# Marking runs of nodes with four bfloat16 operations on VectorE instead of one fp32 operation, in a graph network kernel

## The reference

```python
h = relu(layernorm(x))                                          # (50000, 128)
rel_in = concat([h[src_edges], h[dst_edges], edge_attr], -1)    # (25000, 384)
rel = relu(rel_in @ re_w1 + re_b1) @ re_w2 + re_b2              # (25000, 128)
agg = segment_sum(rel, dst_edges, num_segments=50000)           # (50000, 128)
out = x + relu(concat([h, agg], -1) @ ea_w1 + ea_b1) @ ea_w2 + ea_b2
```

## Time and profile before

| | |
|---|---|
| median of 3 runs | 955.37 us (955.33 to 955.7) |
| the profiled execution | 956.01 us, of which the span of the trace is 954.1 us |
| PE busy | 923.3 us (97%) |
| DVE busy | 740.1 us (78%) |
| ACT busy | 605.5 us (63%) |
| POOL busy | 609.1 us (64%) |
| granted clock of PE, mean | 0.987 |

### The profile page before, as it was taken

How to read it: one execution, slowest core, us unless ns; L and a number is a source line. 1 busy time by engine, 2 the same in 40 slices (tenths; PEclk the granted TensorE clock), 3 DMA queues, 4 the chain that set the end, 5 groups by cost and what they waited for, 6 DMA issues and landing times.

```text
span 954.1 us, 21049 instructions
## 1 busy us (share of the span) xinstructions
PE 923.3 (97%) x6450; PEld 817.8 (86%) x6450; DVE 740.1 (78%) x2155; ACT 605.5 (63%) x1180; POOL 609.1 (64%) x600
## 2 busy tenths in 40 slices
PE   4879999999999999999999999999999999999987
PEld 4668998898898899889889889988988988998876
DVE  5887788788788878878877887886887788788562
ACT  1447666666666766666666676666666667666653
POOL 7785776776677677677667767767766776772320
PEclk7979999999999999999999999999999999999999
DMA  6253655555565565555556556555555655554442
GB/s 200 75 148 113 183 163 168 150 177 175 151 186 168 151 183 163 168 151 176 172 155 185 167 153 183 162 169 158 169 174 151 186 167 152 169 177 146 124 123 76
DMA packets 114105, 151.88 MB, mean 159 GB/s; under 512 B 17984, under 2 KB 70080, under 8 KB 113984
## 3 DMA queue, kind: packets, MB, share of 16 engines
q1 hardware_dynamic: 101440, 124.73, 43.2%
q0 software_dynamic: 12544, 25.72, 10.2%
HBM read 104.92 MB, written 45.46 MB: 158 GB/s over the span
## 4 chain that ended last, share of the span: by engine, by line
PE 94%; DVE 3%; SPq 1%; issue 1%; ACT 1%; DMA 0%; DVEq 0%
PE l_ps L531 33%; PE l_ps L546 27%; PE l_ps L536 17%; PE agg_ps L496 7%; PE edge_ps L479 4%; PE node_ps L487 4%; PE node_ps L471 1%; SPq L294 0%; DVE rel_row L831 0%; DVE hot L844 0%; SPq L300 0%; DVE lo L804 0%; DVE h L797 0%; DMA drow_i<-in_dst_rows 0%; DMA win<-rel_rows 0%
## 5 line engine op out<-in xcount | busy, mean ns | idle before, releaser
L386 POOL DMA_INDIRECT gath<-in_x,dst_all x196 | 200.2, 1022 | 59.7 <-issue 59.7
L386 POOL DMA_INDIRECT gath<-in_x,src_all x196 | 195.0, 995 | 52.9 <-issue 51.7
L546 PE MATMUL l_ps<-w2n,hid 128*128 128x128 f32 x1568 | 193.6, 277 | 0.0
L655 ACT ACTIVATE hid<-l_ps,b1n 128x512 f32<-128x512 f32 x196 | 135.0, 689 | 82.4 <-PE l_ps L536 82.4
L409 POOL TENSOR_TENSOR ea_lo<-ea_in,ea_hi 128x512 fp32r<-128x512 f32 x45 | 74.3, 1651 | 171.6 <-ACT ea_hi L629 171.6
L546 PEld LDWEIGHTS l_ps<-w2n,hid 128*128 128x128 f32 x1568 | 182.9, 192 | 0.1
L810 DVE SCALAR_TENSOR_TENSOR lo<-node_ps,hi 128x512 fp32r<-128x512 f32 x98 | 67.3, 687 | 146.1 <-ACT hi L638 146.1
L663 ACT ACTIVATE h<-xin,shift,rs 128x128 f32<-128x128 f32 x392 | 165.2, 486 | 0.0
L531 PE MATMUL l_ps<-hi,w1n_hi 128*128 128x512 f32 x392 | 155.7, 397 | 0.4 <-ACT hid L655 0.4
L531 PE MATMUL l_ps<-hi,w1n_lo 128*128 128x512 f32 x392 | 155.4, 396 | 0.0
L402 POOL TENSOR_TENSOR xb<-xin,b2n 128x512 f32<-128x512 f32 x98 | 131.0, 1354 | 33.5 <-DVE res L838 33.5
(11 more groups left out here) (98 smaller groups left out, 1566.1 us busy)
## 6 DMA issues: line engine op xcount, KB each, us to landing
win<-rel_rows SPq DMA_DIRECT2D x392, 98.0 KB
xin<-in_x_tiles SPq DMA_DIRECT2D x98, 256.0 KB, 4.2
out<-res SPq DMA_DIRECT2D x98, 256.0 KB, 3.4
rel_rows<-rel_row SPq DMA_DIRECT2D x49, 392.0 KB, 2.4
ea_in<-in_ea_t SPq DMA_DIRECT2D x49, 256.0 KB, 3.2
gath<-in_x,src_all POOLq DMA_INDIRECT x196, 2.7
gath<-in_x,dst_all POOLq DMA_INDIRECT x196, 2.9
w1e<-in_L_gnn_re_w SPq DMA_DIRECT2D x1, 384.0 KB, 3.6
```

Of the source, the lines that this page charges most:

```text
L386: nc.gpsimd.indirect_dma_start(gath[b][:, s, k, :], None, x, bass.IndirectOffsetOnAxis(ap=idx[:, e * T + k:e * T + k + 1], axis=0)).then_i ...
L546: last = nc.tensor.matmul(l2_ps[turn % 2][:, k * P:(k + 1) * P], hid[r][:, c, k * P:(k + 1) * P], w[:, c, :], start=(c == 0), stop=(c == C ...
L655: nc.scalar.activation(hid[r][:, c, :], l1_ps[c][:, :], ACT.Relu, bias=b[:, c:c + 1]).then_inc(hid_set, 1)
```

## The change

The single operation of a mark over 128x512 elements becomes four over 128x128. Before, the inputs were the fp32 row `node_no` (0 to 511) and the destination column spread over the elements; now the input is a bfloat16 row `run_no` (0 to 127), the column of one window is a scalar operand, and the offset `k * P` goes into the added constant. `run_no` is made once, at the start, by a cast from `node_no`. Only the fourth operation raises `hot_set`.

```diff
+        run_no = sb("run_no", [P, P], BF16)
...
             def mark(r, j):
                 dve.wait_ge(win_loaded[r], 16 * T * (j + 1))
                 wait(dve, win_used[r], j)
-                nc.vector.scalar_tensor_tensor(out=hot[r][:, :, :], in0=tiled(node_no), scalar=float(tile_no(r, j) * G),
-                                               in1=win[r][:, :, AT:AT + 1].to_broadcast([P, T, P]),
-                                               op0=ALU.add, op1=ALU.is_equal).then_inc(hot_set[r], 1)
+                if j == 0 and r == 1:
+                    dve.wait_ge(run_no_set, 1)
+                for k in range(T):
+                    last = nc.vector.tensor_scalar(hot[r][:, k, :], run_no[:, :], float(tile_no(r, j) * G + k * P),
+                                                   win[r][:, k, AT:AT + 1], ALU.add, ALU.is_equal)
+                last.then_inc(hot_set[r], 1)
...
             nc.vector.tensor_copy(dst_f[:, :], dst_all[:, :]).then_inc(dst_cast, 1)
             split_weights(1)
+            dve.wait_ge(consts, 8)
+            nc.vector.tensor_copy(run_no[:, :], node_no[:, 0:P]).then_inc(run_no_set, 1)
```

More of the change, by code:

```diff
@@ L145, in gnn_program @@
         dst_cast = sem("dst_cast")
+        run_no_set = sem("run_no_set")
         gathered = [[sem(f"gathered{b}_{k}") for k in range(T)] for b in range(2)]
```

## The result

The changed kernel takes 999.3 us (median of 4 runs, 998.62 to 999.89), the kernel before in the same comparison 955.54 us: 1.0451 times as long, 95% interval 1.0439 to 1.0464. Predicted were 998 us.

What follows compares the result with a forecast made beforehand. PE was taken to bound the kernel. Span 954.1 + 0.5 outside the joint steps + 42 of stalls = 996.6, with 1.9 around it 998.5; 0.6 above the median, so 998 us. Range 960 to 1015 us.

Steps and rivals of the forecast that it cites:

- PE bounds the joint steps: Joint steps: PE is busy 821.00 of 821.00 us from 75 to 896 us, so any wait of PE is seen whole.
- the second marks: Second mark of a joint step: would end at 175.81, PE wants it at 176.39; no cost, even with 1.09 us.
- The price of an operation: One new 128x128 bfloat16 operation on DVE: 0.26 us, four 0.77 us against 0.68; bounds 0.65 to 1.09.
- The estimate of 94 ns for one: Errata table's price of one small DVE operation, 0.38 us for four; the prediction called it too low.
- POOL comes between the operations: First mark, joint steps: each of POOL's three operations comes between two of the four marks; stall 0.95 us, bounds 0.7 to 1.4.
- Three of the four take over 1 us: Sign in the profile after: about three marks per joint step over 1 us, the others near 0.25.
- the 42 that I named as a sign: Sign: PE waits of about 1 us for `hot` in 44 joint steps, some 42 us in total, at `agg_ps`.
- How often: Joint steps: `ea_lo` runs on POOL 45 times, the first slips through, 44 stall; 44 x 0.95 = 42 us.
- the rival of a falling clock: Joint steps: each stall lowers PE's granted clock, 44 add 75 us, giving 1073 us; chance 0.03.
- Outside the joint steps: At `enter` and the last mark, 3 x 0.09 = 0.3 us, plus 0.2 for the `run_no` cast: +0.5 us.
- The weakest step: Joint steps: POOL gets in between two operations that DVE has back to back, the basis of the 0.95 us stall.
- one event: Two fp32 `h` from 552.68 took 1.68 us together, with POOL's `ea_lo` starting inside them and waiting 0.04 us at most.

Runs made afterwards that it cites:

- two pieces: The kernel before, its mark cut into two scalar_tensor_tensor operations of 128x256: 957.79 us in one run.

## Why the prediction was right

**PE bounds the joint steps, and the first mark has 3.16 us behind `ea_lo`.** Right: PE's waits for marks there are new, the second marks (0.73 us) cost nothing, and first marks that were complete within 3.00 us (two pieces) or 2.91 (one POOL operation moved) made PE wait for nothing.

**The price of an operation.** 0.26 us and 0.77 for four were predicted, 0.24 and 0.73 measured. The estimate of 94 ns for one, by the table of the Trainium skill, VectorE: DVE Perf Modes, section on the TRN2 errata, was far too low. That section's rule that each operation pays a fixed cost agrees with the runs: 0.24 us in bfloat16 becomes only 0.27 in fp32.

**POOL comes between the operations.** Right in the outcome: 3.97 us from the start of `ea_lo` to the end of the mark (predicted 4.08), 4.11 to PE's start (predicted 4.13), a stall of 0.95 us (predicted 0.95), a step of 113.69 - 94.39 = 19.30 us. The order inside was not as I had it. I let the first operation go ahead of `ea_lo`, as the old mark did from 0.01 us behind, and hold it up. In fact the first waits as well, and POOL isn't held up (1284 ns, where I expected near 1.4 us). That the stall is 0.95 us to the digit is luck. POOL ends 0.27 us sooner than I had it; then two operations of the mark end behind the last `xb`, not one, which costs 0.15; and PE starts 0.15 us behind the mark's end, not 0.05. In either order all three of POOL's operations precede the fourth. Three of the four take over 1 us, as I had named, but the first is one of them and the fourth is not. (In 2 of the 45 steps the last `h` waits in place of one of them.) PE's recorded waits are 37 us in the 45 steps, not the 42 that I named as a sign, for the reason given with the timeline.

**How often.** I excluded the first joint step, where the mark had been 0.6 us ahead. In the changed kernel's trace it is not ahead (75.10 against `ea_lo` at 75.09), and it stalls too: 45 steps, 45 x 0.95 = 42.8 us. The windows up to the first `ea_lo` and from there to the last, with 44 of the 45 stalls, before and after (columns as in the earlier trace rows):

```profile
0.00:76.00 76.00, 54.21 (x277) 43.80 (x278) 57.46 (x194) 27.86 (x55) 54.75 (x71) 0.84 0.51 147
76.00:883.19 807.19, 807.19 (x5722) 719.30 (x5721) 648.92 (x1892) 541.88 (x1056) 541.26 (x521) 1.00 0.56 165
```

```profile
0.00:75.09 75.09, 51.26 (x278) 40.70 (x279) 58.15 (x200) 28.02 (x56) 54.80 (x70) 0.89 0.51 147
75.09:924.91 849.82, 813.91 (x5720) 717.55 (x5719) 784.70 (x2157) 544.18 (x1056) 498.08 (x521) 1.00 0.54 157
```

The second stretch is 42.6 us longer, 0.97 a step. The granted clock in the joint steps is 1.00, so the rival of a falling clock did not come true.

**Outside the joint steps.** 0.5 us were predicted. The two spans differ by 42.6 us, the medians by 43.8. With 42.6 + 0.95 = 43.6 us in 45 steps the spans leave -1.0: the stretch ahead of the first `ea_lo` is 0.9 us shorter, at a mean granted clock of 0.89 against 0.84. The predicted 0.5 us can't be seen beside that.

**The weakest step** was that POOL gets between any two DVE operations back to back, which rested on one event. It holds for one-input operations with a scalar operand, in bfloat16 and in fp32 (45 of 45 steps each), a form like that event's. As a general rule it is wrong: the two-input form kept POOL out in 29 of 45 steps, with and without a wait of POOL for the first piece; without one it let POOL in only where its first piece had itself waited for `ea_lo` (15 of 15). The reason that I give, that an operation of 0.17 us that needs little of it for its elements leaves a gap in which POOL comes in, while the old form's fills most of its 0.20, fits the counts; it was argued and not shown by itself. With POOL let go behind the first piece, why the old form keeps it out in 29 steps and not in the other 16 stays open.

## What to carry to other kernels

Before an operation of DVE is cut into pieces, look at what POOL does at that place. If the two exclude each other there, each piece can wait for a whole POOL operation, so the price can be that of as many POOL operations as there are pieces, as long as POOL has them ready, and not the pieces' own. What exceeds the room before the result is wanted (3.16 us here) is lost. The sign of it in a profile is a greatest duration far above the median whose end follows a POOL operation's end by the time of the elements alone. Where the order can be chosen, a semaphore that lets POOL start behind the piece that is waited for cost nothing here (1.0003 times the time before).

## What was not expected of the hardware

Busy time of DVE counts this waiting: 140 us more of it, about 5 of them work of the marks. When both start almost together, the form of the operation made the difference here: one of 128x512 with two inputs that starts 0.01 us behind POOL's went first, and so did the first of four two-input pieces of 128x128 that starts 0.03 us behind (337.45 against 337.42); a bfloat16 one of 128x128 with one input that starts 0.01 us behind did not (94.40 against 94.39, 1.33 us). A mark that comes later waits in the old form too: 0.25 us behind, it took 1.59. And POOL's gathers don't take part: four marks beside them take 0.73 us.
